# The experts' routing chain moved behind the first strong expert's hidden blocks in the programs of ACT and DVE

## The reference, cut to what matters

```
h = x @ W_in + b_in                              # 3125 x 256
for l in range(3):
    agg    = segment_sum(h[src], dst) / deg
    logits = concat([h, agg]) @ router_W[l] + router_b[l]      # 8 experts
    vals, idx = top_k(logits, 2); gates = softmax(vals)        # 0 for the other six
    weak   = relu(agg @ weak_W[l] + weak_b[l])                 # 4 weak experts, 256 x 256
    sh     = relu(agg @ strong_W1[l] + strong_b1[l])           # 4 strong ones, 256 x 512
    strong = sh @ strong_W2[l] + strong_b2[l]                  # 512 x 256
    conf   = sigmoid(h @ conf_W[l] + conf_b[l])
    h      = h + conf * sum_e gates_e * expert_e
out = x + h @ W_out + b_out
```

## Time and profile before

| | |
|---|---|
| median of 3 runs | 3267.45 us |
| the profiled execution's own time | 3268.28 us |
| span, first to last instruction | 3265.8 us |
| mean granted TensorE clock | 0.971 |
| PE busy | 2968.8 us (91%) |
| DVE busy | 2186.7 us (67%) |
| ACT busy | 897.4 us (27%) |

### The profile page before, as it was taken

How to read it: one execution, slowest core, us unless ns; L and a number is a source line. 1 busy time by engine, 2 the same in 40 slices (tenths; PEclk the granted TensorE clock), 3 DMA queues, 4 the chain that set the end, 5 groups by cost and what they waited for, 6 DMA issues and landing times. The chain is left out here.

```text
span 3265.8 us, 47549 instructions
## 1 busy us (share of the span) xinstructions
PE 2968.8 (91%) x18761; PEld 1780.3 (55%) x18761; DVE 2186.7 (67%) x4024; ACT 897.4 (27%) x1685; POOL 16.7 (1%) x23
## 2 busy tenths in 40 slices
PE   2888779999897999999979999989999998999997
PEld 2566445555343554545545665655656564656665
DVE  7999445555326777776657666686667586666676
ACT  3888422111111000000023222233222233222222
POOL 2000000000000000000000000000000000000000
PEclk8999989999998999999989999999999999999999
DMA  5455247676004655554330000020000002000001
GB/s 125 147 149 160 82 143 224 219 225 196 22 1 138 175 153 167 166 160 126 100 114 3 4 3 4 3 81 4 3 7 4 3 17 69 3 4 3 4 3 41
DMA packets 310958, 265.84 MB, mean 81 GB/s; under 512 B 32767, under 2 KB 289409, under 8 KB 308174
## 3 DMA queue, kind: packets, MB, share of 16 engines
q1 hardware_dynamic: 296558, 259.28, 25.9%
q10 hardware_dynamic: 13760, 2.61, 0.4%
q0 software_dynamic: 416, 0.85, 0.1%
HBM read 172.67 MB, written 90.05 MB: 80 GB/s over the span
## 5 line engine op out<-in xcount | busy, mean ns | idle before, releaser
L1708 PE MATMUL psum<-r_wd,r_h 128*128 128x512 fp8e4 (+1 forms) x2600 | 568.0, 375 | 13.7 <-ACT r_h L229 13.4
L2283 PE MATMUL psum<-m_agg,m_weights 128*128 128x512 f16 (+2 forms) x2016 | 422.0, 362 | 33.3 <-ACT m_agg L2190 33.3
L2244 PE MATMUL psum<-counts,m_h 128*128 128x512 fp8e4 (+2 forms) x2100 | 417.5, 355 | 12.6 <-DVE m_h L1987 12.6
L2302 PE MATMUL psum<-m_weights,x_nodes 128*128 128x256 f16 (+1 forms) x3600 | 413.0, 273 | 17.0 <-DVE m_wtmp L2097 15.4
L1708 PEld LDWEIGHTS psum<-r_wd,r_h 128*128 128x128 f16 x2600 | 241.5, 97 | 307.5 <-issue 15.5
L2302 PEld LDWEIGHTS psum<-m_weights,x_nodes 128*128 128x128 f16 (+1 forms) x3600 | 350.1, 98 | 74.7 <-DVE m_wtmp L2097 22.1
L2283 PEld LDWEIGHTS psum<-m_agg,m_weights 128*128 128x128 f16 x2016 | 196.8, 101 | 241.2 <-issue 49.3
L2244 PEld LDWEIGHTS psum<-counts,m_h 128*128 128x128 f16 x2100 | 206.3, 98 | 210.3 <-issue 21.3
L2202 ACT ACTIVATE m_hT<-m_hT,m_g 128x256 f32<-128x256 f32 x300 | 135.4, 500 | 599.1 <-DVE m_hT L2111 599.1
L2190 ACT ACTIVATE m_agg<-psum,x_nodes 128x512 f32<-128x512 f32 (+2 forms) x336 | 236.3, 716 | 143.7 <-PE psum L2283 113.7
L2111 DVE SCALAR_TENSOR_TENSOR m_hT<-psum,x_nodes,m_bias 128x512 f32<-128x512 f32 (+1 forms) x150 | 112.0, 750 | 169.8 <-PE psum L2319 169.7
(11 more groups left out here) (298 smaller groups left out, 3275.6 us busy)
## 6 DMA issues: line engine op xcount, KB each, us to landing
r_wd<-packed_sym SPq DMA_DIRECT2D x120, 640.0 KB, 4.1
packed_counts<-strip SPq DMA_DIRECT2D x21, 1800.0 KB, 7.8
sym_blocks<-packed_counts SPq DMA_DIRECT2D x88, 384.0 KB, 4.6
packed_sym<-sym_blocks SPq DMA_DIRECT2D x84, 384.0 KB, 3.3
w_stage<-in_L_gnn_strong_W SPq DMA_DIRECT2D x12, 1024.0 KB, 6.7
m_weights<-in_L_gnn_strong_W SPq DMA_DIRECT2D x21, 512.0 KB, 4.7
x_parked<-x_nodes SPq DMA_DIRECT2D x2, 1600.0 KB, 5.9
x_nodes<-x_parked SPq DMA_DIRECT2D x2, 1600.0 KB, 6.3
```

Of the source, the lines that this page charges most:

```text
L1708: m = pe.matmul(bank[pair[b]][:, 0:2 * cw], h16[:, part, p0 + i, :], f_[:, 2 * b:2 * b + 2, :], start=(p0 + i == 0 and part == 0), stop=(p ...
L2244: m = pe.matmul(bank[kb][:, 0:cw], h16[:, part, i, kb * P:(kb + 1) * P], A[:, i, c_:c_ + cw], start=(i == 0 and part == 0), stop=(i == NT ...
L2283: m = pe.matmul(bank[4 + hh % 2][:, 0:cw], w_[:, i, kb, f * P:(f + 1) * P], agg16[:, j, kb, 0:cw], start=(x_ == 0), stop=(x_ == len(todo) ...
L2302: m = pe.matmul(bank[b_][0:r_, 0:H], s_[:, pa[0] * BANK + k * P:pa[0] * BANK + k * P + r_], w_[:, pa[1], f, :], start=(f == 0 and pa == PA ...
```

## The change

In the loop over chunks, in DVE's program and in ACT's, the call of `route(ci)` and the call of `hidden(ci, 0, range(FB))` change places. PE's and SP's programs stay as they are. In chunk 0 the weight splits stay behind both.

```diff
@@ dve_layer
                     for ci in range(NCH):
                         more = ci + 1 < NCH
                         ts = tiles_of(CH[ci])
+                        hidden(ci, 0, range(FB))
                         route(ci)
-                        hidden(ci, 0, range(FB))
                         if ci == 0:
                             for k in range(FIRST, NPC):
                                 split_low(k)
```

## The result

The changed kernel takes 3287.01 us in the median of 5 runs (3285.05 to 3288.67), against 3267.18 for the one before, timed beside it: 19.8 us more, ratio 1.0057, 95% interval 1.0042 to 1.0072. The forecast was 3272.4 with a range to 3284: right in direction (slower was as likely as no difference), too small by 15 us, and outside the range by 3. The profiled executions, 3268.28 and 3285.35 us, differ by 17.1.

What follows compares the result with a forecast made beforehand. PE bounds chunks 1 to 5 with a stall in it, DVE bounds chunks 0 and 6 after the first blocks. -16.7 + 13.3 + 3.6 + 4.7 = +4.9 us gave 3272.4 us for the median, range 3260 to 3284.

Steps and rivals of the forecast that it cites:

- The fall follows the routing matmuls and not the stall, so I keep the count: Chunks 1 to 5: six of 15 stay at the lower clock, nine do not, giving 16.7 us gained.
- The terms by themselves: Chunks 1 to 5 at full clock: 1.6 us gained with 512 columns, 2.0 with 384; slow chunks have almost nothing to gain.
- Forecast -16.7 us: Chunks 1 to 5, three layers: 4 x 1.6 + 5 x 2.0 + 0.3 us gained.
- My bounds for the count: Chunks 1 to 5: 8 us gained with ten slow chunks, 27 us with none.
- The other signs I had named: Edges 5.2 or 3.9 us after blocks; chunk 0 waits four to five us for L2097; chunk 6 over 2 us.
- Chunk 0: Weight splits come behind the chain, 4.6 us later: 13.3 us lost over three layers, plus 3.6 of clock behind PE's wait.
- The keeps are no earlier: Chunk 0 at the lower clock: ACT's keeps wait for PE, so block 3's split still ends near 2236.15.
- not 0.2 to 0.4: Chunk 0, layers 0 and 2: clock returns about 1 us earlier, so splits end 0.2 to 0.4 us sooner.
- Chunk 6: No edges cover the chain, so DVE reaches L2111 1.5 us late: 4.7 us lost in three layers, bounds 3 and 5.5.
- the clock behind the long wait in chunk 0: After PE's wait of about 4.7 us the clock stays low: 1.2 us each, 3.6 in three layers (0 to 6.2).
- the lower clock takes the gain: Rival: falls hidden in the stall are now paid; 10 of 15 chunks slow, +16 us, 3283.6 us; chance 0.17.

Runs made afterwards that it cites:

- e5: e1 plus, in chunks 1 to 5, PE's routing matmuls cut in two by block 0 of strong expert 0; 3243.11 us, ratio 0.9927 to before.
- e7: The changed kernel with PE's routing matmuls cut in two by block 0 in all chunks; 3273.31 us, ratio 1.0014 to before.
- e2: The kernel before with the new order only in chunk 0 of each layer; 3286.47 us, ratio 1.0058 to before.
- e3: The kernel before with the new order only in chunk 6 of each layer; 3273.25 us, ratio 1.0014 to before.
- e9: The kernel before with extra small DVE instructions behind the gates in chunk 0 of each layer; 3279.62 us, ratio 1.0041 to before.
- e1: The kernel before with the new order only in chunks 1 to 5 of each layer; 3257.34 us, ratio 0.9966 to before.
- e8: The changed kernel with 20 idle matmuls on zeros where PE waits for L2097 in chunk 0; 3276.24 us, ratio 1.0024 to before.
- e4: The kernel before, but ACT alone keeps blocks 0 and 1 ahead of its Exp in all chunks; 3274.73 us, ratio 1.0018 to before.
- e6: The kernel before with PE's routing matmuls cut in two by block 0 in all chunks; 3318.64 us, ratio 1.0164 to before.

## Why the prediction was wrong

**The step that failed** is "The fall follows the routing matmuls and not the stall, so I keep the count". That the fall follows the routing matmuls is right (e5, e7). That the count stays does not follow: e2, with the middle chunks untouched, had nine falls where before had six. Over the traces of kernels with the chain in front in the middle chunks (before, e2, e3, e9) the count is 6, 9, 6 and 7, with it behind (after, e1, e8) 9, 9 and 7, with three long ones each time against none or one. With one trace of each it isn't shown how much of 6 against 9 is the change and how much the execution; a count from a single trace was not a number to keep. After has nine, three of them long. The terms by themselves were right: a clean chunk of 512 columns fell from 74.72 to 73.12 us (1.6 forecast), of 384 from 68.51 to 66.47 (2.0), a slow one of 512 stayed at 74.8. But six chunks were clean, not nine, and a long fall costs 1.7 us beyond the old stall. Forecast -16.7 us, measured -8.9 (e1, the middle chunks alone, gained 11 us by its ratio). My bounds for the count (8 to 27 us of gain) held it. Together with chunk 6 below this is the miss of the traced execution: 7.8 and 5.2 us, less 0.6 in chunk 0, 12.4 in sum, against 12.2 us between the forecast for the profiled execution and its time. The other signs I had named (where the edges start, the wait of 4.7 us, the waits in chunk 6) came as written.

**Chunk 0** came out right, forecast 13.3 of lateness and 3.6 of clock, 16.9, measured 16.3, but that is partly luck: the parts were off against each other. PE goes on 3.0, 4.6 and 2.9 us later in the layers (10.5, not 13.3), and the other 5.8 us are clock. "The keeps are no earlier" is right for layer 1 alone. In layer 0 of the kernel before, PE stood in a stall here too, for ACT's keeps, which came behind a table load and the Exp:

```profile
1709.22 1.28 ACT L2180 ACT_TABLE_LOAD   x1 [6.01 <-issue]
...
1711.45 2.76 PE L2283 MATMUL psum<-m_agg,m_weights 128*128 128x512 f16 x12 [1.18 <-ACT m_agg L2190]
```

After the change that stall is gone and block 3's split ends 1.6 us sooner from the first routing matmul, not 0.2 to 0.4. In layer 2 the half clock at the blocks lasted 6.8 us before and 3.4 after.

The Trainium skill's page "TensorE: Matmul & The Clock Gate", section "HAM oscillation — how this bites in real kernels", says that idle gaps make the array throttle again and that avoiding them keeps it fast. The waits of 3.0 us and more in e9 and in chunks 0 of after, and e8's filled one, agree. In the middle chunks there was no gap of over 0.9 us ahead of the fall: PE had been at work on 9-column matmuls when the clock fell to 0.50, and with that stretch cut in e5 it fell at one chunk of 15.

**Chunk 6** was mis-sized: 4.7 forecast, 9.9 measured. The lateness is as worked out, PE goes on 1.5 us later after L2097 (15.31 us from the chunk's first routing matmul before, 16.85 after), 4.6 in three layers. The other 5.3 us are clock again: in layers 1 and 2 a fall of 3.4 us begins right behind the longer wait, and at the start of layers 1 and 2 the stretch at half clock is 10.2 us, not 6.8. I had priced the clock behind the long wait in chunk 0 and put it at nothing behind this one of 2.5 us. How much of this the change brings each time is open: the same wait of 2.5 us was followed by a fall in 7 of 12 cases (after 2 of 3, e3 none, e7 all, e8 2), e3's ratio shows the lateness alone, 4.6 us, and the 10.2 us stand also in e4, where PE goes on behind L2097 in chunk 6 no later than before.

**The chances.** The rival "the lower clock takes the gain" had its mechanism right and 0.17, at 3283.6. Its price for the count of falls was fair; it lacked the falls of chunk 6. The forecast and this rival should have been one case with a wide size, reaching to 3290.

**What stays open.** Medians differ by 19.8 us and the profiled executions by 17.1; 2.7 us is not assigned, nor is the rest by which e1 to e3 do not add. What exactly decides whether a given chunk meets a fall was not tried beyond the cut and the fill, and no kernel was traced twice, so how the number of falls varies from execution to execution is not known. A version that also helps chunks 0 and 6 was not tried.

## What to carry to other kernels

When a small serial chain is moved behind work that feeds the bound engine, ask stage by stage what else stands behind the chain: here it was hidden where 6.8 us of matmuls followed, and was paid whole where weight splits or the next consumer stood behind it, so the swap belongs in the middle chunks only. Price a stall on TensorE with its clock: here a stall hid a stretch at half clock, and removing it only uncovered that stretch. Break up runs of tiny matmuls by putting full ones between them before counting on the gain, but only where nothing waits for their result: in the middle chunks, with the new order, the two edits together gave 25 us, where the first alone gave 12; with the old order the same cut cost 53 us (e6).

## What the runs showed of the hardware

- With the routing matmuls of 9 columns in one run, 3.6 or 2.7 us of PE "busy", the granted clock fell to 0.50 at 6 to 11 of 15 chunks (56 of 72 with the longer run, 8 of 48 with the shorter); cut into two runs by one block of full matmuls, at 1 and 0 of 15 (e5, e7). With the cut and a stall of 2.7 to 2.8 us close behind it was 10 of 15 again (e6).
- A chunk of 512 columns takes the same 74.8 us with a fall of 3.4 us and no stall as 74.7 with a stall of 1.4 us and no fall.
- Twenty matmuls on zeros in a wait of 4.7 us kept the clock at 1.00 and saved 5.6 us over three places (e8).
- Ten DVE instructions, 2.2 us in all, three times in a kernel of 3267 us, cost 14 us (e9; 9 to 18 by the interval).
